# Two graph-attention layers on one core: a front stage with a column-tiled decay product, loads for two groups, four row buffers and edge rows ahead of the roots

## The reference, cut to what matters

```python
Q, K, V = x @ Wq, x @ Wk, x @ Wv                                # one row per node
denom_t = max(1, edge_type.max() + 1)
dec_in = concat([edge_time[:, None], edge_type[:, None] / denom_t])  # two features per edge
decay = exp(decay_scale * tanh(relu(dec_in @ Wd1 + bd1) @ Wd2 + bd2))  # 2 -> 64 -> 8 heads
m = proj(expmap(x, c), c)                                       # a scale per node from its norm
q_dst = Q[dst] + rel_q[type];  k_src = K[src] + rel_k[type];  v_src = V[src] + rel_v[type]
# later, per edge: logits from q*k*decay and |m[src]-m[dst]|*decay, softmax over dst, weighted sum of v
```

## Time and profile before

| what | value |
| --- | --- |
| median of 3 runs | 3118.83 us (3118.01 to 3123.6) |
| profiled execution, its own time | 3128.77 us |
| its span | 3127.0 us |
| busy in the span: PE, DVE, ACT, POOL | 77%, 76%, 44%, 59% |
| granted TensorE clock, mean | 0.893 |
| end of `front` (first instruction of `edges0` on DVE) | 315.61 us |

### The profile page before, as it was taken

How to read it: one execution, slowest core, us unless ns; L and a number is a source line. 1 busy time by engine, 2 the same in 40 slices (tenths; PEclk the granted TensorE clock), 3 DMA queues, 4 the chain that set the end, 5 groups by cost and what they waited for, 6 DMA issues and landing times. The chain is left out here.

```text
span 3127.0 us, 48874 instructions
## 1 busy us (share of the span) xinstructions
PE 2414.5 (77%) x11946; PEld 1876.9 (60%) x11946; DVE 2361.8 (76%) x5829; ACT 1376.4 (44%) x4161; POOL 1853.1 (59%) x1957
## 2 busy tenths in 40 slices
PE   4887699999999999996688856677677777767644
PEld 3666577777777777775434335666666666656543
DVE  7434799999999999998566636677777777777768
ACT  1433355555555555553255543344433433343307
POOL 1000777777777777773500057777777777777374
PEclk8899899999999999997799978888888888888865
DMA  5277777777777777773101143333333333333131
GB/s 114 55 198 208 208 205 204 202 204 205 205 203 203 206 205 203 203 205 112 21 20 26 26 95 84 84 85 84 82 82 77 83 84 84 84 84 84 31 63 42
DMA packets 253628, 387.14 MB, mean 124 GB/s; under 512 B 70853, under 2 KB 168881, under 8 KB 249642
## 3 DMA queue, kind: packets, MB, share of 16 engines
q0 software_dynamic: 86432, 239.62, 29.6%
q1 hardware_dynamic: 132662, 130.96, 16.6%
q10 hardware_dynamic: 34260, 13.43, 1.8%
HBM read 342.88 MB, written 40.92 MB: 123 GB/s over the span
## 5 line engine op out<-in xcount | busy, mean ns | idle before, releaser
L1826 POOL DMA_INDIRECT pair<-d_table,pair x884 | 841.1, 951 | 566.2 <-POOLq L204 297.0
L1094 POOL DMA_INDIRECT pair<-d_table,index x884 | 843.5, 954 | 276.3 <-issue 253.6
L1993 PE MATMUL e_p_x<-pair,iden 128*128 128x264 f32 x884 | 335.4, 466 | 308.7 <-issue 236.0
L1302 PE MATMUL e_p_x<-big,e_oht 128*128 x1768 | 454.5, 380 | 0.0
L1951 ACT COPY pair<-e_p_r 122x264 f32<-122x264 f32 x442 | 165.6, 375 | 633.3 <-PE e_p_r L2020 629.1
L1854 DVE SCALAR_TENSOR_TENSOR e_prod<-e_p_x,e_att 128x512 f32<-128x512 f32 x221 | 152.9, 692 | 297.4 <-PE e_p_x L1995 262.7
L1302 PEld LDWEIGHTS e_p_x<-big,e_oht 128*128 128x128 f32 x1768 | 336.8, 191 | 46.1
L1993 PEld LDWEIGHTS e_p_x<-pair,iden 128*128 128x128 f32 x884 | 155.5, 219 | 341.9 <-issue 292.5
L1995 PEld LDWEIGHTS e_p_x<-big,e_oht 128*128 128x128 f32 x1768 | 326.5, 229 | 44.5
L1995 PE MATMUL e_p_x<-big,e_oht 128*128 x1768 | 327.0, 316 | 0.0
L1292 PE MATMUL e_p_t<-e_wbd,e_feat 128*128 128x512 f32 x442 | 240.9, 627 | 92.9 <-DVE pair L1146 61.6
(11 more groups left out here) (364 smaller groups left out, 4213.4 us busy)
## 6 DMA issues: line engine op xcount, KB each, us to landing
e_node<-d_node SPq DMA_DIRECT2D x28, 960.0 KB
e_node<-d_node SPq DMA_DIRECT2D x111, 240.0 KB
d_table<-tab_kmv SPq DMA_DIRECT2D x54, 360.0 KB
pair<-d_table,index POOLq DMA_INDIRECT x884
pair<-d_table,pair POOLq DMA_INDIRECT x884, 2.5
e_feat<-in_edge_attr ACTq DMA_DIRECT2D x442, 16.0 KB
e_feat<-in_edge_attr SPq DMA_DIRECT2D x442, 16.0 KB
e_gate<-d_gate SPq DMA_DIRECT2D x84, 64.5 KB
```

Source lines behind the costliest of these rows:

```text
L1094: nc.gpsimd.indirect_dma_start(rows[:, c % RQ0 * QS + t, 0:3 * D], None, k.d_table0, bass.IndirectOffsetOnAxis(ap=k.index0[:, c * QS + t:c ...
L1302: last = M(x[:, t, :], oht[c % 3][:, t * P:(t + 1) * P], qm[:, bass.ds(of[t], 1), :], start=False, stop=True, skip_group_check=True)
L1826: nc.gpsimd.indirect_dma_start(rows[:, r, :], None, k.d_table1, bass.IndirectOffsetOnAxis(ap=index1[:, c * QS + t:c * QS + t + 1], axis=0))\
L1993: M(x[:, 2 * h:2 * h + 2, 0:W], k.iden[:, :], rows[:, r + 2 * h:r + 2 * h + 2, :], start=True, stop=False)
```

## The change

The second product goes to four column tiles of 32: weights `w2` are two blocks of 32 columns instead of eight of 128, each matmul writes the 32 partitions of its column tile, and two of them (one per half) add up. So the tiles of a group are dealt out in another order, four apart, and the loads follow it. A load now serves two groups: three feature buffers (`PT`) hold two groups each. `kmv` has four buffers (`KT`). Blocks start in slot 24 and spread over 30 slots, 24 to 53, so that the last two slots carry blocks alone (`MORE = 2`) and a slot has one or two blocks. The transposes move to slot 21. On VectorE `norms` is cut in two: its second half, now `tangents`, follows `edge_rows`; ScalarE takes the sines behind group 21. The zeroing of the sums moves from the start of `edges0` into `rows`, behind block 8.

```diff
-    PER = 2
-    FROM = NGR - NBP // PER
-    XT, FT = 6, 4
+    NPR = math.ceil(NGR / 2)
+    FROM, MORE = 24, 2
+    XT, FT, PT, KT = 6, 4, 3, 4
-    w2 = cut([P, 8, P])
+    w2 = cut([P, 2, 32])
-    feat = [cut([RB + 5, QS * P]) for u in range(FT)]
+    feat = [cut([RB + 5, 2 * QS * P]) for u in range(PT)]
-    kmv = [sb(f"kmv{u}", [BN, 2, 3, D]) for u in range(2)]
+    kmv = [cut([BN, 2 * 3 * D]).rearrange("p (y a d) -> p y a d", y=2, a=3) for u in range(KT)]
     def blocks(j):
-        return range((j - FROM) * PER, (j - FROM) * PER + PER) if j >= FROM else ()
+        slots = NGR + MORE - FROM
+        return range((j - FROM) * NBP // slots, (j - FROM + 1) * NBP // slots) if j >= FROM else ()
...
-            while stored < C - 1 and stored * (P // TG) + 12 <= FROM + b // PER:
+            while stored < C - 1 and stored * (P // TG) + 12 <= group_of(b):
...
     def first_vector(dve):
-        for t in range(8):
+        for p in range(2):
             for a in range(2):
-                s = 8 * a + t
-                v.did(V.tensor_copy(w2[a * HID:(a + 1) * HID, t, s * H0:(s + 1) * H0], wd2[a * HID:(a + 1) * HID, :]))
+                s = 2 * p + a
+                v.did(V.tensor_copy(w2[a * HID:(a + 1) * HID, p, s * H0:(s + 1) * H0], wd2[a * HID:(a + 1) * HID, :]))
...
         dve.sem_inc(toact, 1)
+
+    def tangents(dve, v):
+        V = nc.vector
         dve.wait_ge(fract, 1)
...
     def rows(dve, emptied):
-            u = b % 2
+            u = b % KT
-            if b >= 2:
-                dve.wait_ge(row_out[u], 16 * (b // 2))
+            if b >= KT:
+                dve.wait_ge(row_out[u], 16 * (b // KT))
             last.then_inc(row_made, 1)
+            if b == 8:
+                V.memset(k.acc0, 0.0)
...
+        def load(J):
+            u, t0 = J % PT, J * 2 * TG
+            if J >= PT:
+                act.wait_ge(hidden, 2 * (J - PT) + 2)
+            for p, a, w in loads(J):
+                o = p * RB
+                if a is None:
+                    act.dma_start(feat[u][o:o + 2, :].bitcast(I32), io["meta"][t0:t0 + 2 * TG, 4 * P:5 * P]
+                                  .rearrange("(i f) e -> f i e", f=4)[2 * p:2 * p + 2, :, :]).then_inc(feat_in[u], 16)
+                    act.dma_start(feat[u][o + 2:o + 4, :], k.d_typet[t0:t0 + 2 * TG, :]
+                                  .rearrange("(i f) e -> f i e", f=4)[2 * p:2 * p + 2, :, :]).then_inc(feat_in[u], 16)
...
-        for j in range(NGR):
-            if j >= 1 and j - 1 + FT < NGR:
-                load(j - 1 + FT)
+        for j in range(NGR + MORE):
+            if j >= 2 and j % 2 == 0 and j // 2 - 1 + PT < NPR:
+                load(j // 2 - 1 + PT)
...
-            if j == 12:
+            if j == FROM - 3:
                 act.wait_ge(toact, 2)
                 A.activation(n["th_n"][:, :], n["z"][:, :], ACT.Tanh)
...
     def on_tensor(pe, edges, edge_major):
-            for t in range(8):
-                p, q = t // QS, t % QS
-                last = M(p_d[j % 2][:, 0:P], w2[:, t, :], hid[j % 2][p][:, q * P:(q + 1) * P], start=(t == 0), stop=(t == 7))
+            for p in range(2):
+                for q in range(QS):
+                    last = M(p_d[j % 2][32 * q:32 * q + 32, 0:P], w2[:, p, :], hid[j % 2][p][:, q * P:(q + 1) * P],
+                             start=(p == 0), stop=(p == 1), tile_position=(0, 32 * q))
...
                 tab["norms"](dve, v)
                 er["vector"](dve)
+                tab["tangents"](dve, v)
                 tab["scales"](dve, v)
...
 (edges0, vector)
-                v.did(V.memset(acc, 0.0))
```

More of the change, by code:

```diff
@@ L633, in tables0 @@
     vec, toact, fract, prepared, spread_w = (sem(m) for m in ("vec", "toact", "fract", "prepared", "spread_w"))
-    feat_in = [sem(f"feat_in{u}") for u in range(FT)]
+    feat_in = [sem(f"feat_in{u}") for u in range(PT)]
     x_in = [sem(f"x_in{u}") for u in range(XT)]
@@ L639, in tables0, with group_of, loads @@
     projected, q_kept, row_made, scaled_w = sem("projected"), sem("q_kept"), sem("row_made"), sem("scaled_w")
-    row_out = [sem(f"row_out{u}") for u in range(2)]
+    row_out = [sem(f"row_out{u}") for u in range(KT)]
     def blocks(j):
-        return range((j - FROM) * PER, (j - FROM) * PER + PER) if j >= FROM else ()
+        slots = NGR + MORE - FROM
+        return range((j - FROM) * NBP // slots, (j - FROM + 1) * NBP // slots) if j >= FROM else ()
+    def group_of(b):
+        return next(j for j in range(FROM, NGR + MORE) if b in blocks(j))
+    def loads(J):
+        t0 = J * 2 * TG
+        if t0 + 2 * TG <= T:
+            return [(p, None, 2 * QS) for p in range(2)]
+        return [(p, a, math.ceil((T - t0 - 2 * p - a) / 4)) for p in range(2) for a in range(2) if t0 + 2 * p + a < T]
     def early(sp):
@@ L686, in on_sync @@
             stored += 1
+        for u in range(KT):
+            sp.wait_ge(row_out[u], 16 * ((NBP + KT - 1 - u) // KT))
         for u in range(2):
-            sp.wait_ge(row_out[u], 16 * (NBP // 2))
             sp.wait_ge(step_out[u], 16 * ((C + 1 - u) // 2))
@@ L692, in first_gpsimd @@
     def first_gpsimd(pl):
-        for u in range(FT):
+        for u in range(PT):
             nc.gpsimd.memset(feat[u], 1.0).then_inc(prepared, 1)
@@ L786, in rows @@
             last.then_inc(row_made, 1)
+            if b == 8:
+                V.memset(k.acc0, 0.0)
     def on_scalar(act, typet_out, emptied):
         A = nc.scalar
[L791 to L800, removed]
-                    continue
[L802 to L807, removed]
+        def load(J):
[9 more added lines that the diff above has]
+                                  .rearrange("(i f) e -> f i e", f=4)[2 * p:2 * p + 2, :, :]).then_inc(feat_in[u], 16)
+                    continue
+                of = slice(t0 + 2 * p + a, t0 + 2 * p + a + 4 * (w - 1) + 1, 4)
+                act.dma_start(feat[u][o + a:o + a + 1, 0:w * P].bitcast(I32), io["meta"][of, 4 * P:5 * P]).then_inc(feat_in[u], 16)
+                act.dma_start(feat[u][o + 2 + a:o + 3 + a, 0:w * P], k.d_typet[of, :]).then_inc(feat_in[u], 16)
         def hidden_layer(j):
@@ L819, in store @@
                 .then_inc(decay_out[j % FT], 16)
-        act.wait_ge(prepared, FT)
+        act.wait_ge(prepared, PT)
         act.wait_ge(typet_out, 16 * 5)
-        for j in range(FT):
-            load(j)
+        for J in range(min(PT, NPR)):
+            load(J)
         hidden_layer(0)
-        for j in range(NGR):
-            if j >= 1 and j - 1 + FT < NGR:
-                load(j - 1 + FT)
+        for j in range(NGR + MORE):
+            if j >= 2 and j % 2 == 0 and j // 2 - 1 + PT < NPR:
+                load(j // 2 - 1 + PT)
             if j + 1 < NGR:
@@ L835, in on_scalar @@
                 A.copy(qm[0:BN, b, 0:D], pq[b % 2][0:BN, 0:D]).then_inc(q_kept, 1)
-            if j >= 1:
+            if 1 <= j <= NGR:
                 store(j - 1)
+            if j >= NGR:
+                continue
             act.wait_ge(raw, j + 1)
@@ L860, in hidden_layer @@
         def hidden_layer(j):
-            u = j % FT
-            parts = 4 if (j + 1) * TG <= T else 2 * sum(T - j * TG > t for t in range(0, TG, QS))
-            pe.wait_ge(feat_in[u], 64 * (j // FT) + 16 * parts)
+            J = j // 2
+            u, c = J % PT, j % 2 * QS * P
+            if j % 2 == 0:
+                pe.wait_ge(feat_in[u], 64 * (J // PT) + 32 * len(loads(J)))
             if j >= 1:
@@ L866, in hidden_layer @@
             for p in range(2):
-                last = M(p_h[p][:, :], k.wd1[p * RB:p * RB + 5, :], feat[u][p * RB:p * RB + 5, :], start=True, stop=True, tile_position=(p * RB, 0))
+                last = M(p_h[p][:, :], k.wd1[p * RB:p * RB + 5, :], feat[u][p * RB:p * RB + 5, c:c + QS * P], start=True, stop=True, tile_position=(p * RB, 0))
             last.then_inc(hidden, 1)
@@ L891, in on_tensor @@
                 pe.wait_ge(tanh, j - 1)
[L892 to L894 removed]
+            for p in range(2):
+                for q in range(QS):
+                    last = M(p_d[j % 2][32 * q:32 * q + 32, 0:P], w2[:, p, :], hid[j % 2][p][:, q * P:(q + 1) * P],
+                             start=(p == 0), stop=(p == 1), tile_position=(0, 32 * q))
             last.then_inc(raw, 1)
[L897 removed]
+    return dict(early=early, weights=weights, sync=on_sync, first_gpsimd=first_gpsimd, gpsimd=on_gpsimd, first_vector=first_vector, norms=norms, tangents=tangents, scales=scales,
                 rows=rows, scalar=on_scalar, tensor=on_tensor, banks=[*pq, *pkv])
```

5 lines of the change are left out of this document (2 added, 3 removed).

## The result

The changed kernel takes 3083.3 us (median of 4 runs, 3079.21 to 3089.03), against 3120.1 for the kernel before beside it (4 runs, 3118.01 to 3123.6): a ratio of 0.9882 [0.9863, 0.9901], 37 us faster. The forecast was 3064 in a range of 3040 to 3099. The profiled execution took 3079.21 us, span 3077.4, 49.6 less than the profiled execution before.

The account below looks back on a forecast made before the run. TensorE's groups, ScalarE's load issues and the wait for roots bound `front`; 132 + 27 x 4.1 + 1.3 + 3 + 16.1 = 263 against 318.1, 55 us earlier, so 3074 profiled, median 3064, range 3040 to 3099.

Parts of the forecast that it names:

- block 0: First block of node rows on TensorE: forecast at 132 us against 167.59, bounds 129 and 150.
- the slots: Second part of `front`, groups with blocks: 27 slots of 4.1 us each in the sum.
- the lead of the blocks: Last slots of `front`: a term of 1.3 us in the sum; before, slot 51's blocks ran 1.4 ahead of its product.
- the end: End of `front`, last steps' store, gather and store: 16.1 us kept from slot 51's product to the zeroing row.
- The second product: TensorE, each group: 1.15 us against 1.88 at the upper clock, 2.27 against 3.72 at the lower.
- rival 2: TensorE's second product: the tiles run together, 0.47 us, slots of 3.75, 67 us earlier, 3052; chance 0.15.
- 3.62 a group: First part of `front`, groups alone: mean of 2.97 and 4.27 us, half of the groups at each clock.
- The cover that the prediction named: SyncE's queue ahead of the first block: x loads landing 10.7 us after the joins and entry at 118 hide the roots' work.
- 4.1 a slot: Second part: 3.46 us of TensorE plus 0.65 for clock dips and waits; bounds 3.5 and 4.9.
- 3 for the zeroing: VectorE behind block 8: of 6.18 us of moved zeroing 3 are lost, bounds 0 to 6.2.
- Rival 4: Second part: TensorE, with less to do, stays at the lower clock, 6.8 us a slot, up to 3151; chance 0.05.
- the prediction's signs of being wrong: In `front`: product of 1.8 us, features late lot after lot, second-part clock below 0.8, block 0 past 150.

Follow-up runs that it names:

- experiment 6: Changed kernel with VectorE's old order restored: the roots' work ahead of the edge rows, sines behind group 12; 3096.45 us, ratio 0.9908 to the kernel before.
- experiment 2: Changed kernel with the column-tiled second product issued twice in the 21 groups ahead of the transposes; 3091.69 us, ratio 0.9914 to the kernel before.
- experiment 7: Changed kernel with a lot's four load issues spread over both slots of a pair; 3077.38 us, ratio 0.9845 to the kernel before.
- experiment 4: Changed kernel with the zeroing of the sums put back to the start of the edge stage; 3078.32 us, ratio 0.9872 to the kernel before.
- the fastest run: Changed kernel with early x loads and emptied, zeroing back, loads spread from slot 20, two extra full-width matmuls a slot; 3054.28 us, ratio 0.9794.
- experiment 1: Changed kernel with the second product's weights back to eight blocks of 128 columns; 3090.97 us, ratio 0.9925 to the kernel before.
- experiment 8: Changed kernel with early x loads and emptied, and full-width second products in the 21 groups ahead of the transposes; 3087.23 us, ratio 0.9882.

## Why the prediction was right, and where its sizes were off

**The sum.** It put the mark of the earlier trace rows, the zeroing, 55 us earlier, at 263. Its place in the changed kernel is 273.7 (271.25 + 2.48, the distance before), so 44.4. The missing 10.6 are block 0 (3), the slots (3.2), the lead of the blocks (0.2) and the end (4.2). The forecast then took the median of before less 55; the profiled executions differ by 49.6, the medians by 37, since the one lay 9 us above its median and the other 4 below. So of the 19 us between 3064 and 3083 10.6 are missing at this mark; about 5 come back behind it, and the other 13 or so are the choice of the two executions.

**The second product** was the step that failed: 0.57 us against 1.15, 1.01 against 2.27. The four column tiles ran together, 1.88/0.57 = 3.3 times as fast. It was rival 2's product. The ground for 1.15, that the hidden layer's two row tiles show no overlap, was a misreading: that its time halves with the clock holds for streams that run together as well as for streams in a line. The row that tells them apart is one product of 512 columns by itself, in the edge stage; TensorE in order of time, at a granted 1.00 (304 to 314.85 us):

```profile
307.10 1.02 PE L1310 MATMUL e_p_t<-e_wbd,e_feat 128*128 128x512 f32 x2
307.95 0.59 PE L1318 MATMUL e_p_x<-pair,iden 128*128 128x256 f32 x2
```

It takes 0.85 us, and 0.86 in the trace of the kernel before (347.57 to 348.43). Two in a line would be 1.70; the hidden layer's two take 1.05, so its row tiles did overlap, unless products over 5 rows stream faster than over 128, which no row here tests. They stood for rival 2 and not against it. A pass of 128 columns then takes 0.85/8 = 0.106 and not 0.058, and nearly all of the 0.118 is stream. The rule quoted there from the Trainium skill ("TensorEngine Tiling (Array Packing)", section "Key Properties") agrees with the 0.57 and with the row tiles' 1.05.

**That rival's time did not follow**, because the product no longer set the pace: in the first part hidden and Relu make 3.37 a group, and SyncE's joins set block 0; in the second the clock fell.

**First part.** 3.62 a group was forecast as a mean over both clocks, beside late features; it was (108.12 - 32.96 - 1.98)/21 = 3.48, with all groups at the lower pace. That is luck: the product was priced too high, and the clock too high as well. First product 34 (32.96), edge rows 71 (71.15), features late 4 us (1.98) were right. Transposes came at 108 instead of 114, and nothing of it was gained: joins forecast to land in 14 us took 16.9, and x loads, forecast from the transposes on (18), started behind `emptied` at 123.31. The cover that the prediction named (118 + 10.7) was in fact the path; it came out 6 us late. Of the 29 us by which the edge rows moved, experiment 6 shows that 12 are due to the order (83.13 against 71.15): the rest would have come with the faster groups, since the roots are taken behind group 11.

**Second part.** 4.1 a slot and 3 for the zeroing gave 113.7, or 4.21 a slot; measured are 136.55 to 253.47, 116.9, or 4.33. The size is near, the reasons are not. Row-store waits fell below 25 us as forecast (1.4), and the transfers did not take their place: where the clock was up a slot of two blocks took 3.12 with TensorE never idle (146.39 to 149.51), and 5.87 at the lower level (193.07 to 198.94). Rival 4 had the mechanism: TensorE with less to do spends more time at the lower level, 0.77 against 0.94. It needed three slots in four there to decide; it got under half. A granted clock below 0.8 in the second part stood among the prediction's signs of being wrong, and it came. The rule quoted in the prediction from the Trainium skill's page "TensorE: Matmul & The Clock Gate", Part 1, that activity releases the throttled state, points the same way, and the run with extra matmuls (1.00) agrees with it; experiment 2 does not by itself, where 33 us without a gap released nothing. The prediction's remark that its best stretches are its busiest does not follow from the earlier trace rows: TensorE was busy 17.06 of 20 us at 0.60 and 21.45 of 26 at 1.00. What TensorE did before the clock fell: at 190 it had been idle for 1.44 us, at 235 for 4.35, both for a late Relu; at 156 it had only a gap of 0.50 behind it, and a gap of 1.37 at 181 did not bring it down. So waits go with the falls without explaining each, and experiment 7, with fewer waits at the same 0.77, says the same. Relu was late for ScalarE's load issues; ScalarE in order of time, beside a DMA share of 0.93 (180 to 190 us):

```profile
184.95 0.59 ACTq L816 DMA_DIRECT2D pair<-d_typet  x1
185.57 0.38 ACTq L814 DMA_DIRECT2D pair<-in_meta  x1
185.98 1.43 ACTq L816 DMA_DIRECT2D pair<-d_typet  x1
187.51 0.60 ACT L828 ACTIVATE pair<-tab_p_h 128x512 f32<-128x512 f32 x1 [2.46 <-PE tab_p_d L911]
```

The eight issues of the last, partial lot took 5.7 us in a row (228.77 to 234.44), and TensorE's wait of 4.35 stands behind them. The prediction had counted issues and not what an issue costs beside full transfers.

**Zeroing** cost about the 3 forecast by the trace (TensorE idle for 3.59) and gained nothing in the edge stage, as forecast (experiment 4).

**End of the stage.** 16.1 us were kept, 20.3 came (253.47 to 273.7). The last blocks did not run beside it for nothing: the last store of decays is issued behind a q copy, 1.24 us after its Exp starts (0.43 before), its landing took 4.9 us (3.5 before) and the gather 7.2 (4.2), beside the last six row stores. That the stores are the cause was read from the trace and not tried.

**What each part is worth** (ratios, in us of 3120): four row buffers 17, column tiles 13, the order 8, the zeroing -3; 35 of the 37, each good to some 9 us by the intervals of its two ratios. So by the times only the buffers and the tiles can be told from no effect, and that the sum comes so near is no evidence. The loads for two groups and the 30 slots were not undone alone; their share stays open.

**Luck.** The time lies in the range, but several terms behind it were wrong and cancel: a product half as long as forecast, against joins that land later and a clock that falls.

## What to carry to other kernels

When an engine's work shrinks, look first for what it was covering: here a queue's wait for a small transfer and an engine's load issues. Then price its new load at the clock it will have; a faster product that leaves TensorE at the lower level gives back much of what it saves. Extra full-width work can hold the clock and still gain no time, as four matmuls a slot did; two were in the fastest run, untried by themselves. And a row that halves with the clock says nothing of overlap: look for the same product by itself. A median over executions whose clock differs is the honest measure; one trace of such a stage is a sample.

## What the runs showed of the hardware

- Sixteen passes with 32 columns of weights on four column tiles: 0.57 us; with 128 columns: 1.88. The hidden layer's two products of 512 columns on two row tiles: 1.05, against 0.85 for one such product over all 128 rows.
- In the first part the record grants 1.00 from 57 to 103 us, while hidden takes 2.00 as it does at a recorded 0.50. There the durations decide; in the second part record and durations agree, and in experiment 1, where the upper level had been reached by 50 us, already in the first (0.68 from 67 to 77, hidden 2.00 at 71.45).
- Three transfers of joins took 16.9 us to land, behind the small stores of the edge rows' ends in the queue (13.9 before, 13.2 in experiment 6; why was not tried): SyncE's queue moved 0.02 MB in 2967 packets from 94 to 118 us, and the DMA share was 1.06 at 34 GB/s (100 to 108 us).
- In experiment 8 single load issues on ScalarE took 2.20 and 3.75 us at a DMA share of 0.09 (106 to 114 us). Why stays open.
